# A transformer layer on one Trainium2 core: the scores in three parts on 128, 64 and 32 rows of TensorE

## What is computed

```python
def _L0_attn_ref(queries, Wq, Wkv, Wout, bout):
    q = queries @ Wq
    k, v = jnp.split(queries @ Wkv, 2, axis=-1)
    q, k, v = (split_heads(q), split_heads(k), split_heads(v))
    q, k = (_rope(q), _rope(k))
    sim = jnp.einsum('bhid,bhjd->bhij', q, k) * SCALE
    attn = jax.nn.softmax(sim, axis=-1)
    out = jnp.einsum('bhij,bhjd->bhid', attn, v)
    out = out.transpose(0, 2, 1, 3).reshape(b, n, HEADS * DIM_HEAD)
    return out @ Wout + bout
x = L0_attn_queries
x = x + _L0_attn_ref(_layernorm(x, axis=-1), ...)
x = x + _L0_ffn_ref(_layernorm(x, axis=-1), ...)   # gelu((x U1) V1 + b1) U2 V2 + b2
```

## Time and profile before

| | |
|---|---|
| median of 3 runs | 1569.16 us (1568.19 to 1571.64) |
| the profiled execution | 1572.87 us |
| its span, first to last instruction | 1570.9 us |
| busy: TensorE | 1443.6 us, 92% |
| busy: ScalarE | 1063.3 us, 68% |
| busy: GpSimd | 988.6 us, 63% |
| busy: VectorE | 942.3 us, 60% |
| busy: the 16 DMA engines, queue 1 | 21.5% |

### The profile page before, as it was taken

One profiled execution on the slowest core, in us unless ns is written; L12 is line 12 of the kernel. 1 busy time (PEld: TensorE's weight loads), 2 busy tenths in 40 slices (PEclk: granted clock), 3 DMA queues, 4 the chain that ended last, 5 costly groups with the idle time before them and its releaser, 6 DMA issues.

```text
span 1570.9 us, 29110 instructions
## 1 busy us (share of the span) xinstructions
PE 1443.6 (92%) x7289; PEld 541.1 (34%) x7289; DVE 942.3 (60%) x1809; ACT 1063.3 (68%) x2024; POOL 988.6 (63%) x517
## 2 busy tenths in 40 slices
PE   3698999999999999999999999999999999998886
PEld 1133333333324333333424333332433333343323
DVE  7465665566565656656566566656665665657444
ACT  2476776677767677767767776767767676776564
POOL 4389856658485665748476575848566574848631
PEclk9699999999999999999999999999999999999999
DMA  5412131221303122220313122130312222031002
GB/s 149 86 31 54 33 80 23 57 58 38 77 14 79 27 60 51 56 59 14 79 36 75 27 57 58 26 80 24 79 23 59 56 52 63 14 79 37 1 15 67
DMA packets 76421, 80.76 MB, mean 51 GB/s; under 512 B 29252, under 2 KB 43080, under 8 KB 76072
## 3 DMA queue, kind: packets, MB, share of 16 engines
q1 hardware_dynamic: 74880, 78.89, 21.5%
q10 hardware_dynamic: 1448, 1.00, 0.3%
HBM read 22.56 MB, written 2.36 MB: 16 GB/s over the span
## 4 chain that ended last, share of the span: by engine, by line
PE 73%; issue 8%; ACT 7%; POOL 5%; DVE 5%; ACTq 1%; DMA 1%; SPq 0%; DVEq 0%; POOLq 0%
PE O L399 26%; PE S L387 13%; PE S L388 11%; PE MD L408 10%; PE TILE L319 4%; PE TILE L337 4%; PE TILE L313 3%; PE TILE L329 2%; ACT OS L504 2%; ACT PF L532 2%; ACT LEFT L517 2%; POOL SA L706 2%; DVE STAGE L556 1%; ACT STAGE L443 1%; POOL WRAW L299 1%
## 5 line engine op out<-in xcount | busy, mean ns | idle before, releaser
L706 POOL TENSOR_TENSOR SA<-PF 128x1024 f32<-128x1024 f32 x256 | 623.0, 2442 | 434.6 <-DVE SUM L633 292.2
L625 DVE CUSTOM_DVE_ANT_0 LEFT<-MR,LEFT 128x512 f32<-128x512 f32 x512 | 353.3, 690 | 481.8 <-ACT LEFT L517 477.1
L532 ACT ACTIVATE PF<-S 128x512 f32<-128x512 f32 x1024 | 553.1, 596 | 44.7 <-PE S L388 35.2
L517 ACT ACTIVATE LEFT<-MD 128x512 f32<-128x512 f32 x512 | 308.3, 602 | 381.8 <-PE MR L409 349.2
L399 PE MATMUL O<-PF,V 128*64 128x512 f32 x2048 | 502.7, 612 | 15.2 <-ACT OS L504 15.2
L387 PE MATMUL S<-QK 128*128 128x512 f16 x1024 | 393.2, 384 | 10.5 <-ACT PF L532 10.5
L388 PE MATMUL S<-QK 128*128 128x512 f16 x1024 | 389.2, 380 | 0.0
L408 PE MATMUL MD<-KD,QK 64*128 64x512 f16 x512 | 225.5, 440 | 15.8 <-ACT LEFT L517 9.1
L636 DVE TENSOR_TENSOR SUM<-SUM,SA 128x1024 f32<-128x1024 f32 x128 | 227.0, 1773 | 8.6 <-POOL SA L706 8.3
L409 PE MATMUL MR<-QK 64*128 64x512 f16 x512 | 225.8, 441 | 0.0
L399 PEld LDWEIGHTS O<-PF,V 128*64 128x64 f32 x2048 | 125.6, 137 | 225.4 <-issue 158.8
(11 more groups left out here) (101 smaller groups left out, 1001.3 us busy)
## 6 DMA issues: line engine op xcount, KB each, us to landing
QK<-STAGE SPq DMA_DIRECT2D x128, 256.0 KB, 3.2
QK<-STAGE SPq DMA_DIRECT2D x128, 128.0 KB, 3.1
RB<-den SPq DMA_DIRECT2D x128, 128.0 KB, 3.0
KD<-KDS SPq DMA_DIRECT2D x128, 32.0 KB, 2.7
X<-in_L_attn_queries SPq DMA_DIRECT2D x4, 512.0 KB, 12.9
RT<-DS SPq DMA_DIRECT2D x128, 2.0 KB, 1.7
out<-X SPq DMA_DIRECT2D x8, 256.0 KB, 2.3
WRAW<-in_L_attn_Wkv SPq DMA_DIRECT2D x1, 1024.0 KB, 8.9
```

The source lines that it names most:

```text
L517: e.activation(LEFT[:, side, :], MD[:, :], ACT.Relu).then_inc(left_over, 1)
L532: e.activation(PF[:, t % SLOTS, z * HALF:(z + 1) * HALF], S[:, bank_of(t, z), :], ACT.Exp, scale=EXP_SCALE).then_inc(exped, 1)
L625: e.tensor_tensor_reduce(LEFT[:, side, :], MR[side][:, :], LEFT[:, side, :], 1.0, LOWEST, ALU.add, ALU.max, MX[:, place % 2, q:q + 1]).the ...
L706: e.tensor_tensor(SA[:, (t // 2) % 2, :], PF[:, t % SLOTS, :], PF[:, t % SLOTS + 1, :], ALU.add).then_inc(two_summed, 1)
```

## The change

The scores of a step are taken apart. High by high and low by high stays one matmul on 128 rows (`KHL` by `QHH`, now in `pe_scores` alone). High by low is a matmul on 64 rows, for the two halves of the queries side by side, on rows 0 to 63 and 64 to 127 (`pe_low`, for both steps of a pair at once). The maximum is four matmuls of one row each, on rows 0, 32, 64 and 96, into the four score banks. `pe_low` stands once in two steps, in the even one, behind the unit and ahead of the scores. `S` has four banks; for that the second bank of `MR` and the second `LEFT` go, so a unit waits for VectorE's maximum of the unit before it. In the twelve units ahead of the loop two idle score banks serve as the second set.

Beside that: `KD` moves into the place of the zeros in `QK` (`KMH[0:64]`), so each of its DMAs carries 128 KB instead of 32 KB and fills rows of `QML` as well. The row of the maxima goes by four DMAs instead of one. One memset replaces three. The copy of `O` moves from ScalarE, third step of a head, to VectorE, fifth step, with `PV_LAG` = 6. Tiles stand in odd steps only, except the sums. VectorE looks at a tile in the tile's own step, ahead of the maximum in odd steps and behind it in even ones, and the sums and norms follow the maximum instead of preceding it. The ScalarE copy of a "rot" tile stands two steps after it instead of three, so in the step of a "pass" tile; GpSimd's `rot_low` stands three steps after it instead of four.

```diff
-PV_LAG = 4
+PV_LAG = 6
-QK_AT = (1, 3, 4, 7, 8, 10, 11, 13)
-KD_AT = 9
-V_AT = {14: (1, 0), 16: (1, 1), 22: (0, 0), 24: (0, 1)}
+QK_AT = (1, 3, 5, 7, 9, 11, 13, 15)
+KD_AT = 10
+V_AT = {17: (1, 0), 19: (1, 1), 25: (0, 0), 27: (0, 1)}
-OUT_AT = {17: (1, 0), 19: (1, 1), 28: (0, 0), 30: (0, 1)}
+OUT_AT = {21: (1, 0), 23: (1, 1), 29: (0, 0), 31: (0, 1)}
...
-        S = pb("S", [P, 3, HALF], F32)
+        S = pb("S", [P, 4, HALF], F32)
         MD = pb("MD", [P, 512], F32)
-        MR = [pb(f"MR{n}", [P, 512], F32) for n in range(2)]
+        MR = pb("MR", [P, 512], F32)
...
+        def pe_low(e, it, t):
+
+            h = t // KT
+            if t % KT == 0:
+                e.wait_ge(max_row, ROWS * (it.i * GH + h + 1))
+            for side in range(2):
+                keys = slice((t % KT + side) * P, (t % KT + side + 1) * P)
+                for z in range(2):
+                    rows, queries = slice(DH * z, DH * z + DH), slice(z * HALF, (z + 1) * HALF)
+                    wait(e, exped, 2 * (it.step(t) + side) + z - 3)
+                    e.matmul(S[:, 2 * side + z, :], (KHL, KMH)[z][rows, h, keys], QML[rows, h, queries],
+                             start=True, stop=False, skip_group_check=True)
+            for b in range(4):
+                row = slice(32 * b, 32 * b + 1)
+                e.matmul(S[:, b, :], MSC[row, :], MQ[row, h, :], start=False, stop=False, skip_group_check=True)
...
+            e.wait_ge(left_over, it.step(u))
+            e.wait_ge(max_read, it.step(u))
+            pe_unit(e, it.step(u), place, q, MD[:, :], MR[:, :])
...
-            for n, kind, args in it.at(t - 3):
+            for n, kind, args in it.at(t - 2):
                 if kind == "proj" and args[2] == "rot":
                     act_rot(e, args, it.i + 1)
...
         def dve_step(e, it, t):
             u = t + LEAD
             h, kt = t // KT, t % KT
-            dve_tiles(e, it, t)
+            if kt == PV_LAG - 2 and (not it.first or h > 0):
+                dve_copy_out(e, it.i * GH + h - 1, (h - 1) % GH)
+            if t % 2 == 1:
+                dve_tiles(e, it, t)
+            if not (it.last and u >= STEPS):
+                dve_max(e, it.step(u), it.i * GH + u // KT, (u // KT) % GH, u % KT, MR[:, :], LEFT[:, :])
+            if t % 2 == 0:
+                dve_tiles(e, it, t)
...
-            if not (it.last and u >= STEPS):
-                dve_max(e, it.step(u), it.i * GH + u // KT, (u // KT) % GH, u % KT, u % 2)
...
-            for n, kind, args in it.at(t - 4):
+            for n, kind, args in it.at(t - 3):
                 if kind == "proj" and args[2] == "rot":
                     rot_low(e, args, it.i + 1)
```

More of the change, by code:

```diff
@@ L617, in split_ff_weights, with dve_max @@
                                    ALU.subtract).then_inc(f_w_lo, 1)
-        def dve_max(e, u, head, place, q, side):
+        def dve_max(e, u, head, place, q, right, left):
             if q == 0:
@@ L832, in _ @@
             pool.wait_ge(powers_set, 1)
[L834 to L836 removed]
+            pool.memset(STAGE[:, 0, :, 512:N], MSCALE).then_inc(set_up, 1)
             pool.memset(ONES[:, :], 1.0).then_inc(set_up, 1)
[L838 removed]
+            pool.wait_ge(set_up, 2)
             ln_rstd(pool, 0)
```

113 lines of the change are left out of this document (52 added, 61 removed).

## The result

The changed kernel takes 1690.93 us (median of 4 runs, 1689.96 to 1692.54) against 1568.68 us before (4 runs beside them): a ratio of 1.078, 95% interval 1.0758 to 1.0803. That is slower, as forecast, but by 122 us instead of 40, and outside the range of 1562 to 1670.

What follows compares the result with a forecast made beforehand. TensorE's stream was taken to bound the kernel before, the maximum's chain the changed one. An iteration of 90.3 + 2.0 + 0.7 + 0.3 = 93.3 us, overlap taking the growth to 2.8, gave +42, -2 outside: 1609 us, range 1562 to 1670.

Steps and rivals of the forecast that it cites:

- small additions: Waits for the copy, GpSimd and hand-over on top of the loop: 2.0 + 0.7 + 0.3 us an iteration, taken as 2.8.
- TensorE's stream: TensorE's own matmuls in a pair of steps: 5.05 us instead of 5.10, dense 84.0 an iteration.
- Rival 3: Row groups don't run side by side, so scores and loop start later in every pair: 1688 or 1765 us; chance 0.13.
- The loop: Even unit through scores, exponentials, n copies, Relu and maximum back to TensorE: 5.09 + 0.5 n us; sum 90.3 an iteration.
- The copy of `O`: On VectorE, behind a sum and ahead of the maximum, it delays odd units: 2.0 us an iteration (bounds 0 and 3).
- GpSimd: Its sums come late for ScalarE's copy of one tile, step 9's: 0.7 us an iteration (bounds 0 and 2).
- The sums tile in step 20: Extra tile on TensorE, adding 1.1 us an iteration; the one in step 6 adds only 0.8.
- The hand-over: SyncE's DMAs after the last `rot_low` land late for the new group's first unit: 0.3 us an iteration (bounds 0 and 1.5).
- Several of these small waits overlap: A pair late for one reason hides the next, so 2.8 us an iteration and +42 us in all.
- Outside the loop: Fewer memsets save about 1 us, first units alternating banks another 1 to 2, partly taken back: -2 us in all.
- The fourth: GpSimd and the hand-over become last: 95 to 98 us an iteration, 1640 to 1690 us; chance 0.12.
- The first two: Loop's cover holds, 1492 us, chance 0.10; or a draw with copy, GpSimd and hand-over free, 1550 to 1570, chance 0.13.

## Why the prediction was wrong

Direction and mechanism held, the sum did not. The step that failed is the one from the loop to the total: the small additions to it, 2.0 + 0.7 + 0.3 an iteration, taken down to 2.8 for overlap. The iteration shown is not 2.8 but 7.1 us longer than before. Without rounding on the way the loop's own terms are 90.1, so 6.9 us came on top of them. By steps of the prediction:

**TensorE's stream: right.** Unit to scores 1.13 us for a forecast of 1.18, a pair with an output tile 5.23 for 5.29. The low pairs cost 0.26 each rather than 0.215, the one-row products with their change of shape 0.33 rather than 0.38. Rival 3 is out: four row groups do run side by side. Where the clock stays full, TensorE is busy 85.1 us an iteration after 86.3, a gain of 1.2 for a forecast of 0.8.

The Trainium skill (TensorE: Matmul & The Clock Gate, Measured speedup vs the span model) has 3.07x for four row tiles; by it these products would take an estimated 0.44 us with the change of shape, where the trace has 0.33.

**The loop: right in its links, short in two.** Behind a wait, the exponentials start 1.73 us after the unit (953.42 to 955.15), not 1.60; and from the maximum's start to TensorE it is 0.85 (958.89 to 959.74), not 0.74, of which 0.05 had no row behind it. That is 0.2 in each pair that waits: 6.32 for a "pass" pair of 6.09, 5.71 and 5.78 for V pairs of 5.59. Over the nine pairs with no other cause it makes 1.3 us an iteration.

**The copy of `O`: right in sum, for other reasons.** I took a sum at its mean of 1.77. While GpSimd adds, it takes 2.1 to 2.7 us (2.23 above), otherwise 1.2 to 1.5. The copy of `O` is 0.69 for each half. So the odd unit of step 5 waits 1.49 us, and its pair takes 6.54, not 5.85. But the pairs of steps 12 and 28 take only 5.41 each, less than with the copy's 0.5 to 0.75. The three together are 1.9 us over the loop; I had 2.0.

**GpSimd: a term mis-sized.** Its lateness I had put at one tile of four and 0.7 us ("for the other three tiles it is in time"). It hits two, at steps 11 and 15, and their pairs are 7.29 and 6.98 us long for a forecast of 6.09. That is 2.1 us:

```profile
886.68 0.63 ACT L472 ACTIVATE STAGE<-YR 128x512 f16<-128x512 f32 x1 [0.93 <-POOL YR L691]
...
899.07 0.63 ACT L472 ACTIVATE STAGE<-YR 128x512 f16<-128x512 f32 x1 [0.64 <-POOL YR L691]
```

**The sums tile in step 20: a term short.** Its pair takes 7.01 us for 5.29 + 1.1. The output tile behind it waits 0.42 us until ScalarE has copied the sums out of the tile bank, a wait that the kernel before does not have.

**The hand-over: a term mis-sized.** I took 0.3 us. Twelve of the loop's fourteen iterations wait 1.08 to 1.18 us for it (the 21.5 us of the whole run include 7.28 ahead of the loop), and the pair of step 18 is then 6.38 long instead of 5.71. The DMAs of 256 KB land after 3.7 us instead of 3.2, and issues take up to 1.29 us in the iteration shown.

**The clock: a term I left out.** In the iteration shown TensorE had waited 1.60 us for the maximum at 901.22, and then its clock stood at the lower of its two levels for most of the next pair. Two stretches (columns as at the top), the unit in the first of them, and the iteration ahead of it with its own wait at the same step and for the hand-over:

```profile
902.00:907.50 5.50, 5.50 (x32) 2.50 (x30) 1.97 (x6) 3.54 (x7) 5.21 (x3) 0.69 0.05 11
907.50:918.00 10.50, 9.44 (x67) 3.82 (x66) 6.21 (x10) 6.90 (x14) 5.30 (x3) 1.00 0.91 193
...
904.96 0.65 PE L416 MATMUL MD<-QK 64*128 64x512 f16 x1
...
773.95:870.87 96.92, 85.07 (x506) 34.03 (x505) 61.45 (x109) 58.43 (x114) 57.97 (x29) 1.00 0.25 55
...
804.30 0.41 PE L416 MATMUL MD<-QK 64*128 64x512 f16 x1 [1.59 <-DVE MX L624]
...
816.46 0.41 PE L416 MATMUL MD<-QK 64*128 64x512 f16 x1 [1.16 <-DMA QK<-STAGE]
```

The granted clock is 0.69 of full in the first stretch, a mixture of 1.2 and 2.4 GHz, and 1.00 in the second. The unit's matmul took 0.65 us instead of 0.43, and this pair 6.61 instead of the 5.78 of the iteration ahead. A wait can thus cost more than its length. But it does so only sometimes: waits of 1.6 us stand at two places of nearly every iteration (steps 12 and 16), and a drop of the clock follows one of them in six iterations of the fourteen. And it costs the iteration little: 97.08 here against 96.92 in the iteration ahead, 97.3 where the drop comes at step 12. Before the change it cost more: not all fourteen iterations take 90.0 us, as I wrote; two take 91.4 and 91.6, at a granted clock of 0.98:

```profile
446.17:537.72 91.55, 87.96 (x441) 32.39 (x441) 54.21 (x101) 63.79 (x123) 57.85 (x30) 0.98 0.21 50
```

**"Several of these small waits overlap, since a pair late for one reason hides the next, so I take 2.8": a discount on terms that were too small.** Such hiding exists: in the iteration shown the slow pair of step 16 took the place of the wait for the hand-over, so that 0.8 us of slow clock cost 0.2. But it is small beside what the terms lacked. Added up, the 6.9 us over the loop's own terms are GpSimd 2.1, the copy of `O` 1.9, the two short links 1.3, the slow clock (or the hand-over in its place) 1.0 and the sums tile 0.6. I had 3.0 for all of them, less 0.2. The bounds that I had given to the copy, GpSimd and the hand-over (3, 2 and 1.5) make 96.8 us with the loop's 90.3, near the 97.08 measured; I used their middle.

**Outside the loop: wrong sign.** The first iteration loses 12 us by its step-20 sums tile (130.66 instead of 118.61), where I had gained about half a microsecond. The earlier start is 0.6 us (first unit at 43.89 instead of 44.47), not 2. Its own maxima wait in the open, 3.24 us for the DMA of the first and 4.82 for a unit at 103.71.

Put together, on the scale of the profiled executions, 1613 was forecast and 1691.6 measured. From that sums tile to the one fourteen iterations on (1387.59 before, 1497.93 after) the loop grew by 98 us, 7.0 an iteration where I had 2.8: 59. The part ahead of it brings 12 to 13, the part behind it, which grew by 8.2, another 7. That is all of the 78.6. The 82 between 1609 and 1691 hold 3 more, since I took off 3.7 for the profiled execution before, and that of the changed kernel lies only 0.6 above its median.

**The rivals.** The fourth, GpSimd and hand-over last with 95 to 98 us an iteration and 1640 to 1690, gave the number (97.08), and had 0.12. That it met the number is in part luck, since it was not the cause by itself: TensorE's largest wait is that for the maximum, 155.8 us. The run without the bank's wait shows the limits within 21 us of each other, which a list of exclusive rivals doesn't hold: I should have added them, not chosen. The first two are out.

**What stays open.** Why the same moves cost 51 us beside two banks is shown only as far as the waits go (Relu behind GpSimd's sum, hand-over), not which tile's step does it. And the 33 us of split scores in the order of the change fit the 0.8 us by which they delay the first exponential, but no run separates delay from burst. How much of the loss in the runs without the bank's wait is the clock's is open too.

## What to carry to other kernels

A second PSUM bank is not a luxury when the reader's answer comes by way of two other engines: add up the whole ring, from the matmul over each queue that its consumers stand in and back, and compare it with the work of one turn before giving the bank away. If the ring is longer, TensorE's savings were worth half or nothing here, and each link's price is its duration beside the neighbour that is busy at that moment, not its mean. Don't take a discount for overlap before the terms themselves are bounded from above. And don't add up what single pieces of a mend gain: two that gained 26 and 5 us alone gave 24 with a third, and adding one that gained 21 alone turned that into a loss of 24.

## What the runs showed of the hardware

VectorE's maximum over two operands takes 0.69 us with one of them in a PSUM bank, in all of the changed kernel's 506 cases (672 to 693 ns), whatever GpSimd does. With both in SBUF the same instruction takes 0.69 us while GpSimd rests and 2.71 in the row below while it works, up to 2.85 in the run. Both rows are of the run in which it read a constant in SBUF, GpSimd's sums from its timeline beside them:

```profile
912.32 0.69 DVE L627 CUSTOM_DVE_ANT_0 LEFT<-ROPE,LEFT 128x512 f32<-128x512 f32 x1 [0.46 <-ACT LEFT L519]
914.44 2.71 DVE L627 CUSTOM_DVE_ANT_0 LEFT<-ROPE,LEFT 128x512 f32<-128x512 f32 x1 [0.28 <-ACT LEFT L519]
...
914.24 5.13 POOL L722 TENSOR_TENSOR SA<-PF 128x1024 f32<-128x1024 f32 x2 [7.61 <-DVE SUM L635]
```

The mean went from 690 to 1253 ns, and that of the adding sums from 1717 to 2207. The Trainium skill (GPSIMD Engine Reference, Specifications) says that GpSimd shares its SBUF interface with VectorE and names instructions with two SBUF inputs as a case of contention. These rows agree, and put the price at up to four times the duration.
